# An adaLN two-layer kernel on one core: a preparing activation taken out, one flip of h brought forward by a tile

## What is computed

```python
x = L0_attn_x                                          # (8, 512, 128)
mod = (silu(c) @ wmod).reshape(8, 6, 1, 128)           # sa, ca, ga, sb, cb, gb; ga and gb kept away from 0
h = layernorm(x) * (1 + ca) + sa
x = x + ga * ssm(h)                                    # state space block with residual and layernorm
h = layernorm(x) * (1 + cb) + sb
f = silu((h @ w1.T) * s1) * ((h @ w2.T) * s2)          # 128 -> 512, "gate" and "up"
f = gelu((f @ h1.T) * sh1)                             # 512 -> 512
f = gelu((f @ h2.T) * sh2)                             # 512 -> 512
x = x + gb * ((f @ w3.T) * s3)                         # 512 -> 128, "y"
# layer 1: gated linear attention (8 heads), then a mixture of LoRA experts: not touched by the change
```

## Time and profile before

| | |
|---|---|
| median of 3 runs | 574.96 us (574.64 to 575.14) |
| the profiled execution's own time | 574.96 us |
| span of that execution, first to last instruction | 573.1 us |
| TensorE busy | 534.0 us, 93% |
| VectorE busy | 389.6 us, 68% |
| ScalarE busy | 346.6 us, 60% |
| GpSimd busy | 196.6 us, 34% |
| TensorE's granted clock, mean over the span | 0.975 of full speed |

### The profile page before, as it was taken

How to read it: one execution, slowest core, us unless ns; L and a number is a source line. 1 busy time by engine, 2 the same in 40 slices (tenths; PEclk the granted TensorE clock), 3 DMA queues, 4 the chain that set the end, 5 groups by cost and what they waited for, 6 DMA issues and landing times. The chain is left out here.

```text
span 573.1 us, 10227 instructions
## 1 busy us (share of the span) xinstructions
PE 534.0 (93%) x3768; PEld 442.4 (77%) x3768; DVE 389.6 (68%) x1013; ACT 346.6 (60%) x630; POOL 196.6 (34%) x261
## 2 busy tenths in 40 slices
PE   8599989989999999899999999999999689999993
PEld 6558867867777788688888888878888578888883
DVE  6986968787777856565858595959596546454431
ACT  4888778768678887466555555554545334455640
POOL 3402430240030021133455454646464514343211
PEclk9789999999999999899999999999999979999997
DMA  8500000000022000000000000000000000001001
GB/s 300 150 2 1 1 0 1 1 2 0 1 88 91 2 0 2 0 2 1 1 1 2 1 1 1 2 3 1 1 1 2 1 1 0 21 19 37 21 19 38
DMA packets 10805, 11.72 MB, mean 20 GB/s; under 512 B 737, under 2 KB 9377, under 8 KB 10625
## 3 DMA queue, kind: packets, MB, share of 16 engines
q1 hardware_dynamic: 9696, 10.50, 5.5%
q10 hardware_dynamic: 1056, 0.52, 0.3%
HBM read 8.92 MB, written 2.10 MB: 19 GB/s over the span
## 5 line engine op out<-in xcount | busy, mean ns | idle before, releaser
L1074 PE MATMUL bank<-ffn_g_hi,w_hi 128*128 128x512 f32 x288 | 116.9, 406 | 0.1
L1075 PE MATMUL bank<-ffn_g_lo,w_hi 128*128 128x512 f32 x288 | 114.1, 396 | 0.0
L1416 DVE TENSOR_TENSOR_SCAN att_decay<-bank,norm_out 128x512 f32<-128x512 f32 x64 | 77.6, 1213 | 34.2 <-PE bank L1872 34.2
L611 DVE TENSOR_TENSOR ffn_g_lo<-ffn_full,ffn_g_hi 128x512 fp32r<-128x512 f32 x96 | 67.1, 699 | 27.2 <-ACT ffn_full L857 25.9
L1880 PEld LDWEIGHTS bank<-att_qT,h_full 128*128 128x128 f32 x512 | 66.9, 193 | 5.3 <-issue 1.6
L1880 PE MATMUL bank<-att_qT,h_full 128*128 128x128 f32 x512 | 68.8, 278 | 0.2 <-DVE att_outer L1448 0.2
L1074 PEld LDWEIGHTS bank<-ffn_g_hi,w_hi 128*128 128x128 f32 x288 | 54.3, 189 | 13.9 <-issue 1.7
L1730 ACT COPY att_qT<-bank 128x512 f32<-128x512 f32 x64 | 37.3, 587 | 44.6 <-PE bank L169 41.4
L1075 PEld LDWEIGHTS bank<-ffn_g_lo,w_hi 128*128 128x128 f32 x288 | 54.3, 189 | 11.7
L1424 DVE TENSOR_TENSOR att_prob<-bank,att_decay 128x512 f32<-128x512 f32 x64 | 42.7, 667 | 21.2 <-issue 16.5
L857 ACT ACTIVATE ffn_full<-bank,cols 128x512 f32<-128x512 f32 x64 | 44.2, 696 | 19.7 <-PE bank L1075 14.5
(11 more groups left out here) (227 smaller groups left out, 1227.1 us busy)
## 6 DMA issues: line engine op xcount, KB each, us to landing
out<-att_vw SPq DMA_DIRECT2D x8, 256.0 KB, 2.3
x<-in_x SPq DMA_DIRECT2D x3, 512.0 KB, 12.4
w_raw<-in_w_all SPq DMA_DIRECT2D x1, 1152.0 KB, 8.9
w_raw<-in_w_all SPq DMA_DIRECT2D x1, 768.0 KB, 10.2
stage<-in_sel SPq DMA_DIRECT2D x1, 640.0 KB, 9.0
v_raw<-in_v_all SPq DMA_DIRECT2D x1, 576.0 KB, 5.8
x<-in_x ACTq DMA_DIRECT2D x2, 256.0 KB, 3.5
w_raw<-in_w_all SPq DMA_DIRECT2D x1, 512.0 KB, 5.4
```

What stands on the lines that cost most here:

```text
L611: dve.tensor_tensor(lo, full[j % 4][:, :], hi.bitcast(F32), ALU.subtract).then_inc(low, 1)
L1074: pe.matmul(acc, w[0], x[0], start=start, stop=False)
L1075: return pe.matmul(acc, w[0], x[1], start=False, stop=stop)
L1416: dve.tensor_tensor_scan(decay[at % ND][:, :], bank("decay", b, k)[:, :], ident4[:, :], 0.0, ALU.mult, ALU.add).then_inc(decay_ready, 1)
```

## The change

It has two parts. (1) The one-element Silu at the end of pairs 0, 1 and 2 is taken out, with its `if`. (2) The flip of sequence e + 2 stands one tile earlier, after tile 16 instead of 17, in TensorE's order and in the bank table, and ScalarE's `bring_h(e + 2)` stands one tile earlier, after gelu 17 instead of 18.

```diff
@@ the bank table, loop_uses @@
-                    if i < 2 and j == 17:
+                    if i < 2 and j == 16:
                         uses.append((("flip", 2 * i + 4), 6))
@@ ScalarE @@
                         if i < 2:
                             if j in (14, 19):
                                 normalise(e + 2 + (j == 19))
-                            if j in (18, 22):
+                            if j in (17, 22):
                                 bring_h(e + 2 + (j == 22))
...
-                    if i < 3:
-                        act.activation(scT[:, 0, 0:1], r["neg_half"][:, 0:1], ACT.Silu)
                     bring_y(2 * i)
```

## The result

| | before | changed |
|---|---|---|
| median, 6 runs each side by side | 574.90 us (574.64 to 575.90) | 578.75 us (577.42 to 579.88) |
| ratio, 95% interval | | 1.0065 [1.0048, 1.0083] |
| span of the profiled execution | 573.1 us | 575.7 us |
| last `bring_y` of the first block starts at | 236.29 us | 240.48 us |

The change makes the kernel slower by 3.85 us, or 2.8 to 4.8 us by the interval of the ratio: 0.7%, small but clear of zero.

A forecast was written before the change was run, and what follows sets the result against it. TensorE, busy 93% of the span, was taken as the bound, held back after pair ends by ScalarE's path. Losses of 4.04 + 0.05 = 4.1 us moved 574.96 to 579.0 us; range 577.0 to 580.5.

The forecast's parts named there:

- The sum: Whole kernel: 4.04 us lost to three table loads plus 0.05 for the moved flip, 579.0 us; chance 0.85.
- nothing gives the delay back: After each pair's end TensorE, ScalarE and VectorE run late by the same amount; 1.42 us at pair 0 stays lost.
- (A): First tiles of a pair: TensorE's queue of four banks swallows part of the delay; half given back, 577.0 us; chance 0.04.
- The reason given at the end of pair 2: ScalarE is late there because it rounds layer 1's weights; `bring_y` gains 0.25 us, leaving 1.19 us lost.
- The moved flip: Flip and `bring_h` of sequence e + 2: gain 0, possible input wait booked at 0.05 us, bounds 0 to 0.4.
- Where TensorE waits: Expected sign: product waits up about 1.3 us at each of three places, plus a new `norm_out` wait of about 1.1.
- (C): TensorE's clock falls at the three pair ends, some 2 us lost each, 585 us; chance 0.04.
- The second block as long as before: Expected sign: the first block ends 4 us later and the second block keeps its length.
- a difference that arises after 240 us: Named sign, no size, that the prediction is wrong: the change's effect appearing after 240 us.
- (B): Load hidden behind `bring_y`, given at least 1.4 us of TensorE and VectorE work before silu 0's use; 574.7 us; chance 0.03.
- (D): Each exposed table switch at the pair ends costs 2.7 us, load plus drain; 583 us; chance 0.02.
- (E): Earlier flip ends the later flip's 3.3 us of waits, and the loads are hidden too; 571.4 us; chance 0.02.

The follow-up runs named there:

- dose: Kernel before plus one ScalarE copy of 128 x 512 numbers behind `bring_y` of pairs 0, 1 and 2: 576.52 us, ratio 1.0020, first block +1.56 us.
- p1_only: Kernel before with only the one-element Silu taken out at the ends of pairs 0, 1 and 2: 579.85 us, ratio 1.0062, first block +4.07 us.
- late_sel: late_flip with the rounding of layer 1's selection matrices moved from pair 2, tile 22, to pair 3, tile 20: 571.10 us, ratio 0.9923.
- p2_only: Kernel before with only the flip of sequence e + 2 and its `bring_h` a tile earlier: 575.57 us, ratio 1.0002, first block -0.03 us.
- silu_first: Kernel before without the one-element Silu, `bring_y` of pairs 0, 1 and 2 behind the next pair's first silu: 575.23 us, ratio 1.0000.
- late_flip: Kernel before with, in pairs 0 and 1, the e + 3 flip after tile 22 and the projection after the first sequence's `y`: 571.91 us, ratio 0.9936.
- late_silu_first: Kernel before with the edits of late_flip and silu_first together: 571.22 us, ratio 0.9940, first block -3.54 us.

## Why the prediction was right, and where it was not

**The sum.** 579.0 us was forecast and 578.75 measured; 4.04 us were booked for the loads, in shares of 1.42, 1.43 and 1.19, and the first block shows 4.06, in shares of 1.41, 1.43 and 1.20. The mechanism was right as well as the number, because one place was followed instruction by instruction: the start of `bring_y` is held by TensorE and does not move, the load does not overlap its neighbours, the first product stood idle for silu 0 and passes all of it on. The step "nothing gives the delay back" is shown by the dose, which returned 0.52 us per end for a shift of 0.50, and by p1_only for the whole load. That the earlier trace rows show only 0.30 us of waiting at the up tile meant no slack on TensorE, not little dependence: rival (A) read it the other way and fell. One sum of the range is off: 579.8 + 0.25 + 0.6 is 580.6 and not 580.4, so the upper end of 580.5 held less than the stated allowances. The measured median is not near it.

**The reason given at the end of pair 2 was wrong,** though its number was right. The prediction said that ScalarE is late there because it rounds layer 1's weights. late_sel shows that rounding hidden, in the kernel with the late flip, which leaves pair 2 as it was. The 0.25 us come from gelu, load and small Silu being longer than `y`.

**The moved flip.** 0.05 us booked, -0.03 measured, in p2_only. The bounds of 0 to 0.4 were too cautious. The weight load in pair 1 waited 0.20 to 0.22 us, but the weight loads there start 0.23 us ahead of their matmuls (116.88 and 117.11 in the changed kernel), so that wait reached nobody; in pair 0 there is none. That the lowering of gelu 17 is hidden was assumed and holds, by the same run.

**Where TensorE waits** was half right. About 1.3 us more of waiting for the product were expected at each end, besides some 1.1 us for the silu. The weight loads' waits on the product grew from 6.4 to 6.9 us only, and those on the silu from 2.1 to 6.0. The two expected waits together, 2.4 us, are also more than the 1.42 us that the prediction itself books for an end; its rival (C) had it right, with 1.1 us at the gate tile and 0.3 more at the up tile. TensorE stops at the gate tile first, and only the remainder is left for the up tile.

**"The second block as long as before"** does not hold for the profiled execution, and this is why its span grew by 2.6 us instead of 4.1. From the last `bring_y` to the end of the span it is 573.1 - 236.29 = 336.8 us before and 575.7 - 240.48 = 335.2 changed. In p1_only, which has the same first block, it is 578.1 - 241.27 = 336.8. In silu_first, whose first block is that of before within 0.13 us, it is 571.7 - 236.46 = 335.2. So the 1.6 us go with the execution and not with the change, although the prediction had named a difference that arises after 240 us as a sign that it was wrong.

They lie where TensorE's granted clock falls to half speed. Counted from the last `bring_y`, the changed kernel is 0.26 us ahead at the end of the first such stretch (13 us on), stays there up to 228 us on, is 0.65 ahead behind the second one (231 us on) and 1.55 ahead after the last eight matmuls of the program. Those eight in the kernel before, in two groups of four (columns as in the earlier trace rows):

```profile
564.00:566.00 2.00, 1.09 (x4) 0.64 (x4) 0.37 (x2) 0.42 (x1) 0.00 (x0) 0.62 0.00 0
566.00:568.00 2.00, 1.11 (x4) 0.93 (x4) 0.63 (x2) 0.16 (x1) 0.00 (x0) 0.50 0.00 0
```

and in the changed kernel, where the clock is still at full speed:

```profile
568.00:570.00 2.00, 1.30 (x8) 0.91 (x8) 0.00 (x0) 0.58 (x1) 0.00 (x0) 1.00 0.00 0
```

The same eight matmuls take 2.20 us there and 1.30 here. Why the clock fell 2 us later in one execution than in the other is not shown. The mean clock of the changed kernel's executions goes from 0.969 to 0.978, with 577.4 to 578.2 us at 0.975 and above and 579.3 to 580.1 at 0.972 and below. The range's allowance of 0.6 us for this was too small for a single execution, not for the median.

**The other rivals.** (B), the load hidden at its new place, needed 1.4 us of work between `bring_y` and silu 0's first use; the dose shows that not even 0.5 us pass unseen. (C), the clock falling at the pairs' ends: in the changed kernel the granted clock is 1.00 from 84 to 90, 136 to 142 and 184 to 192 us, around the three new gaps. (D), a switch that costs 2.7 us: the silu starts 0.01 us after the load's end, and a drain as in the Trainium skill (ScalarE: Activation LUTs, section "What ACT_TABLE_LOAD costs") shows in no row here; the measurement decides. (E) was wrong as a consequence of the change, but its price was real: late_flip took the later flip's waits away and gained 3.60 us, with the projection moved as well.

## What to carry to other kernels

An activation that looks useless may be there to place a table load: before taking one out, look in the built order for where the load goes, and ask whether what then precedes it waits for another engine. Its price is the idle time the load leaves, not the load: 1.2 to 1.4 us per switch where it left 1.2 to 1.3 us of idle time, 0.2 to 0.3 where hardly any was left, none where TensorE is the slower side. And where an engine waits for data for a small step, put the step behind the next tile that does not need them: 3.6 us here, from two moved flips and the projections behind them.

## What the runs showed of the hardware

- A table load need not wait for all that its activation waits for. In the changed kernel's order the first silu waits for two signals; the load ahead of it carries the one of VectorE (`ffn_product_ready`), the silu itself that of TensorE (`front_mm`). In silu_first the load starts 0.02 us after the last gelu and ends 1.53 us before its silu, which TensorE holds up. So there the first activation of a set prefetched its own table, since nothing that waits stood ahead of it.
- Medians of the unchanged kernel in the four batches went from 574.87 to 575.67 us, and single executions from 573.3 to 576.2. Two sources show in the traces: the first Gelu load at 45.0 to 45.2 or at 45.9 to 46.1 us, and 334.9 to 336.9 us from the last `bring_y` to the end. By windows of 2 us, the three shortest ends (changed, silu_first, late_silu_first: 334.9 to 335.2 us) spend 15 to 16 us at half clock, the other eight (336.4 to 336.9) 19 to 22 us. What decides between them stays open. The first block, measured between two landmarks, is free of both, which tells a shift of 0.5 us clearly where the medians cannot tell 1.
